# A graph layer's softmax walk: three groups of edges in flight on VectorE instead of two

## The reference

```python
# layer 0: attention over the edges that end in a node, with softmax
h = x @ W
a_src, a_dst = h @ att_src, h @ att_dst
e = leaky_relu(a_src[src] + a_dst[dst], 0.2)      # self loops are added as edges
m = segment_max(e, dst)
e = exp(e - m[dst])
out = segment_sum(h[src] * e / segment_sum(e, dst)[dst], dst)
x = layernorm(x + tanh(out + bias))
# layer 1: h = gelu(x @ W_pre + b_pre); aggr = segment_sum(h[src] * edge_attr, dst)
#          x = layernorm(x + ((x + aggr) + gelu(gelu((x + aggr) @ W1 + b1) @ W2 + b2)))
```

## Time and profile before

| | |
|---|---|
| timed runs, median | 3724.72 us |
| timed runs, all | 3725.86, 3724.72, 3724.6 us |
| span of the profiled execution, first to last instruction | 3722.8 us |
| its own time | not listed apart from the three; the median is 1.9 us above its span |
| GpSimd busy | 2781.1 us (75%) |
| VectorE busy | 2438.3 us (65%) |
| TensorE matmul busy | 2393.6 us (64%) |
| ScalarE busy | 1283.2 us (34%) |

### The profile page before, as it was taken

The page is one execution under the profiler, slowest core; times in us unless marked ns, Lnnn a source line. Parts: engine busy times, 40 slices in busy tenths (PEclk is TensorE's granted clock), DMA queues, the critical chain, the costliest instruction groups (busy, mean ns, idle before and its releaser), DMA issues.

```text
span 3722.8 us, 66966 instructions
## 1 busy us (share of the span) xinstructions
PE 2393.6 (64%) x16704; PEld 1951.7 (52%) x16705; DVE 2438.3 (65%) x6240; ACT 1283.2 (34%) x3893; POOL 2781.1 (75%) x2950
## 2 busy tenths in 40 slices
PE   6433343434344444444445988989888989999888
PEld 3333333333333333333334777777776777777776
DVE  7444444444466666566666777777777788888886
ACT  5433343434445555555553111111111221111222
POOL 7777777777777777777775777777777777777776
PEclk7555555555555555555557999999999999999998
DMA  5222221222222222222223343443334343444332
GB/s 102 43 42 42 41 44 42 44 42 43 42 43 44 43 44 43 43 44 45 44 45 99 93 94 90 95 94 94 95 91 96 93 96 91 97 95 99 93 95 70
DMA packets 351632, 254.26 MB, mean 68 GB/s; under 512 B 254125, under 2 KB 279218, under 8 KB 351387
## 3 DMA queue, kind: packets, MB, share of 16 engines
q0 software_dynamic: 94016, 146.16, 17.8%
q1 hardware_dynamic: 242753, 99.71, 11.7%
q10 hardware_dynamic: 14618, 6.14, 0.6%
HBM read 244.43 MB, written 7.25 MB: 68 GB/s over the span
## 4 chain that ended last, share of the span: by engine, by line
POOL 60%; issue 24%; ACT 4%; DVE 4%; PE 3%; DMA 2%; ACTq 1%; DVEq 1%; POOLq 0%; SPq 0%
POOL rows L690 60%; ACT onehot L747 1%; DMA rows<-table,src_i 1%; DMA src_i<-in_src_dram 1%; PE bank L1086 1%; ACT L790 1%; ACTq L740 0%; ACT pair L767 0%; DVE score L1361 0%; PE bank L1029 0%; PE bank L962 0%; ACT rowu L796 0%; DVE bst L1399 0%; ACT unused L790 0%; DVE newp L1352 0%
## 5 line engine op out<-in xcount | busy, mean ns | idle before, releaser
L690 POOL DMA_INDIRECT rows<-table,src_i x2850 | 2694.8, 946 | 896.0 <-issue 859.5
L1086 PE MATMUL bank<-node,hot 128*128 128x288 bf16 x9310 | 1228.4, 294 | 28.1 <-issue 16.5
L995 PE MATMUL bank<-onehot,rows 128*97 128x72 f32 (+1 forms) x3048 | 584.9, 369 | 814.9 <-ACT onehot L777 814.9
L1086 PEld LDWEIGHTS bank<-node,hot 128*128 128x128 bf16 x9310 | 932.2, 101 | 282.4 <-issue 20.9
L995 PEld LDWEIGHTS bank<-onehot,rows 128*97 128x97 f32 x3048 | 530.8, 281 | 854.4 <-issue 792.5
L1505 DVE TENSOR_SCALAR hot<-node,key 128x642 bf16<-128x642 int16 x1862 | 870.3, 539 | 130.8 <-PE bank L1086 80.0
L900 ACT ACTIVATE pair<-dst_i 128x8 f32<-128x8 int32 x196 | 35.2, 180 | 1175.3 <-DVE rows L1531 904.3
L747 ACT ACTIVATE onehot<-iota,far_dst 128x72 f32 (+1 forms) x1564 | 384.4, 328 | 23.0
L1339 DVE SCALAR_TENSOR_TENSOR other<-onehot,bank 128x576 f32<-128x576 f32 (+1 forms) x196 | 121.9, 622 | 404.1 <-ACT bank L760 335.4
L1073 PE MATMUL bank<-onehot,rows 128*96 128x40 f32 (+1 forms) x3128 | 306.8, 256 | 88.4 <-DVE rows L1536 50.6
L1073 PEld LDWEIGHTS bank<-onehot,rows 128*96 128x96 f32 x3128 | 295.8, 170 | 110.1 <-issue 88.7
(11 more groups left out here) (204 smaller groups left out, 1931.1 us busy)
## 6 DMA issues: line engine op xcount, KB each, us to landing
attr<-in_edge_attr_dram SPq DMA_DIRECT2D x190, 336.0 KB
rows<-table,src_i POOLq DMA_INDIRECT x2850
node<-in_src_dram SPq DMA_DIRECT2D x195, 64.0 KB
attr<-in_edge_attr_dram SPq DMA_DIRECT2D x190, 48.0 KB
dst_i<-in_dst_dram SPq DMA_DIRECT2D x200, 4.0 KB
src_i<-in_src_dram SPq DMA_DIRECT2D x195, 4.0 KB
src_i<-in_src_dram SPq DMA_DIRECT2D x190, 3.5 KB
dst_i<-in_dst_dram SPq DMA_DIRECT2D x190, 3.5 KB
```

The lines of the kernel that those rows point to most:

```text
L690: pool.indirect_dma_start(rows[:, u, j * width:(j + 1) * width], None, table, bass.IndirectOffsetOnAxis(ap=src_i[:, u, j:j + 1], axis=0))\
L995: last = pe.matmul(total[:, 0:w], rows0(u, it)[:, j, 0:D1], wide(weights, w)[:, j, :], start=j == 0, stop=j == most - 1)
L1086: last = pe.matmul(p_got[t], hot[:, c % HOTS, i, t * P:(t + 1) * P], tab[:, a, :, :].rearrange("p k d -> p (k d)"), start=a == 0, stop=a = ...
```

## The change

Layer 0 only. GpSimd's program is the same; SyncE's differs in one semaphore.
- attend on VectorE is cut in pieces. For group g it now does cand and newp, then top_node of g + 1, drop of g, bent (the max with the slope) of g + 1, the subtract and the peak of g, both operations on acc for g - 1, and then started (L1339, L1309 and L1344 before) of g + 2, where it waits for that group's rows. Three groups lead in before the first round.
- ScalarE's weights does newp, fade and weights of g, then given and sloped of g + 2, then away of g + 3.
- away writes into other, of which there is one, and not into onehot; it therefore waits for t0.shift of the group before its own. score has five slots, in the memory of attr, which layer 0 doesn't need.
- TensorE spreads the maxima of g + 1, sums all tiles of g in one go, and turns the maxima of g + 2. A chunk's work on it stands behind the round.
- SyncE waits for the sum (e0.acc) and not for VectorE's add. The buffers of the branch have names of their own.

```diff
-        score = sb("score", [P, TILES * WIN])
+        score = attr[:, :, :].rearrange("p s n -> p (s n)")[:, 0:SLOTS * TILES * WIN].rearrange("p (u n) -> p u n", u=SLOTS)
...
+        def later(g, it, u, k):
+            if it is ROUNDS or (it is ROUNDS - 1 and u + k > SLOTS):
+                return None
+            return g + k, it + (u + k) // SLOTS, (u + k) % SLOTS
...
-                    sp.wait_ge(e.free, g + 1)
+                    sp.wait_ge(e0.acc if e is e0 else e1.free, g + 1)
...
+                act.wait_ge(t0.shift, g + 1)
                 for j in range(tiles_of(g)):
-                    last = act.activation(wide(onehot[:, u, :], w)[:, j, :], iota[:, bass.ds(lo, w)], ACT.Square,
+                    last = act.activation(wide(other, w)[:, j, :], iota[:, bass.ds(lo, w)], ACT.Square,
...
             def weights(g, it, u, ws):
                 w = ws[0]
-                if g is not LAST and u > 0:
-                    away(g + 1, it + (u + 1) // SLOTS, (u + 1) % SLOTS, ws[1])
-                act.wait_ge(t0.shift, g + 2)
-                act.activation(p_slope(w, tiles_of(g)), by_half(score[:, :], w, tiles_of(g)), ACT.Copy, scale=SLOPE).then_inc(t0.slope, 1)
                 act.wait_ge(t0.newp, g + 1)
                 act.activation(p_newp[:, 0:w], newp[:, 0:w], ACT.Copy).then_inc(t0.newpb, 1)
...
+                if later(g, it, u, 2):
+                    given(*later(g, it, u, 2), ws[2])
+                    sloped(*later(g, it, u, 2), ws[2])
+                if later(g, it, u, 3):
+                    away(*later(g, it, u, 3), ws[3])
...
             def attend(g, it, u, ws):
 
                 w = ws[0]
+                if later(g, it, u, 1):
+                    spread_top(t0, g + 2, ws[1], top_diag, p_topb)
...
-                window_sum(p_acc0, onehot[:, u, :], it, u, range(TILES // 2), w)
-                if u == SLOTS - 1:
-                    due(pe, it, middle)
-                spread_top(t0, g + 2, ws[1])
-                window_sum(p_acc0, onehot[:, u, :], it, u, range(TILES // 2, TILES), w).then_inc(e0.acc, 1)
+                window_sum(p_acc0, onehot[:, u, :], it, u, range(tiles_of(g)), w, tiles_of(g)).then_inc(e0.acc, 1)
+                if later(g, it, u, 2):
+                    turn_top(t0, g + 3)
...
+            def started(st, g, it, u, w):
+                v.wait_ge(t0.away, g + 1)
+                v.wait_ge(t0.given, g + 1)
+                n = tiles_of(g)
+                st.link(v.scalar_tensor_tensor(wide(other, w, n), wide(other, w, n), -1.0,
+                                               over_window(p_src, w, n), ALU.mult, ALU.add))
+                largest(t0, other, w, n)
+                v.tensor_tensor(wide(score[:, u, :], w, n), wide(other, w, n), over_tiles(p_dst[:, 0:w], w, n), ALU.add)\
+                    .then_inc(t0.shift, 1)
+            def bent(st, g, it, u, w):
+                n = tiles_of(g)
+                v.wait_ge(t0.slope, g + 1)
+                st.step(v.tensor_tensor(by_half(score[:, u, :], w, n), by_half(score[:, u, :], w, n), p_slope(w, n), ALU.max))
...
+                candidate(st, t0, g + 1, here, w, p_topb)
+                v.tensor_tensor(newp[:, 0:w], cand[:, 0:w], peak[:, here], ALU.max).then_inc(t0.newp, 1)
                 after = None if g is LAST else load_window(g + 1)
+                if later(g, it, u, 1):
+                    top_node(st, t0, g + 2, ws[1], top_diag)
...
                 st.step(v.tensor_tensor(drop[:, 0:w], peak[0:D1, here], newp[0:D1, 0:w], ALU.subtract))
+                if later(g, it, u, 1):
+                    bent(st, *later(g, it, u, 1), ws[1])
+                v.wait_ge(t0.newpb, g + 1)
+                v.tensor_tensor(wide(score[:, u, :], w, n), wide(score[:, u, :], w, n), over_tiles(p_newp[:, 0:w], w, n),
+                                ALU.subtract).then_inc(t0.score, 1)
...
+                if later(g, it, u, 2):
+                    if first(it) and u + 2 < SLOTS:
+                        score_column(u + 2)
+                    started(st, *later(g, it, u, 2), ws[2])
```

More of the change, by code:

```diff
@@ L664, in body @@
                         pool.wait_ge(s_last, 16)
-                        pool.wait_ge(e.free, LAST + 1)
+                        pool.wait_ge(e0.acc if e is e0 else e1.free, LAST + 1)
                         for j in range(LAST_T):
@@ L783, in weights @@
                         act.activation(fade_x[:, 0:w], drop[:, 0:w], ACT.Exp)
[L784 to L786 removed]
+                        act.activation(onehot_x[:, 0:TILES * w], further_score[:, 0:TILES * w], ACT.Exp).then_inc(tx.w, 1)
+                if later(g, it, u, 2):
[3 more added lines that the diff above has]
+                    away(*later(g, it, u, 3), ws[3])
             act.wait_ge(s_const, 5)
@@ L855, in _ @@
             act.wait_ge(a_peak, CHUNKS + RING)
-            given(0, 0, 0, SLIM)
-            away(1, 0, 1, SLIM)
+            for u in range(2):
+                given(u, 0, u, SLIM)
+                sloped(u, 0, u, SLIM)
+                away(u + 1, 0, u + 1, SLIM)
             def middle_due(it):
@@ L1036, in _ @@
             pe.wait_ge(s_w, 16 * 8)
-            spread_top(t0, 1, SLIM)
-            groups(pe, attend, alone=2)
+            turn_top(t0, 1)
+            spread_top(t0, 1, SLIM, top_diag, p_topb)
+            turn_top(t0, 2)
+            groups(pe, attend, middle_due, alone=2)
             def unread(n):
@@ L1306, in scores, with largest @@
                                                over_window(rows0(u, it)[:, :, D1], w), ALU.mult, ALU.add))
-            def largest(t, w, n=TILES):
-                v.tensor_reduce(top[:, 0:w], other[:, 0:n * w].rearrange("p (j n) -> p n j", j=n), AX.X, ALU.max)\
+            def largest(t, of, w, n=TILES):
+                v.tensor_reduce(top[:, 0:w], of[:, 0:n * w].rearrange("p (j n) -> p n j", j=n), AX.X, ALU.max)\
                     .then_inc(t.top, 1)
-            def shift(st, lo, w):
-                st.step(v.tensor_tensor(wide(score, w), wide(other, w), over_tiles(adst[:, bass.ds(lo, w)], w), ALU.add))
@@ L1315, in top_node, with further_shift @@
-            def top_node(st, t, n, w):
+            def further_shift(st, lo, w):
+                st.step(v.tensor_tensor(wide(further_score, w), wide(further_other, w), over_tiles(adst[:, bass.ds(lo, w)], w),
+                                        ALU.add))
+            def top_node(st, t, n, w, diag):
                 v.wait_ge(t.topt, n)
                 st.link(v.tensor_reduce(top_col[0:w, :], p_top[0:w, :], AX.X, ALU.max))
-                v.tensor_scalar(top_diag[0:w, 0:w], ident[0:w, 0:w], top_col[0:w, 0:1], None, ALU.mult)\
+                v.tensor_scalar(diag[0:w, 0:w], ident[0:w, 0:w], top_col[0:w, 0:1], None, ALU.mult)\
@@ L1333, in attend @@
                 lo, further, prev = window(u, "0_" + named(it, u, ws))
-                st = Steps(v, e0.v, g * STEPS0, STEPS0)
-                v.wait_ge(t0.away, g + 1)
-                v.wait_ge(t0.given, g + 1)
+                st = Steps(v, e0.v, AHEAD0 + g * STEPS0, STEPS0)
                 here = bass.ds(lo, w)
                 n = tiles_of(g)
-                st.link(v.scalar_tensor_tensor(wide(other, w, n), wide(onehot[:, u, :], w, n), -1.0,
-                                               over_window(p_src, w, n), ALU.mult, ALU.add))
@@ L1341, in attend @@
-                largest(t0, w, n)
+                candidate(st, t0, g + 1, here, w, p_topb)
+                v.tensor_tensor(newp[:, 0:w], cand[:, 0:w], peak[:, here], ALU.max).then_inc(t0.newp, 1)
                 after = None if g is LAST else load_window(g + 1)
-                v.wait_ge(t0.w, g + 1)
-                v.tensor_tensor(wide(score, w, n), wide(other, w, n), over_tiles(p_dst[:, 0:w], w, n), ALU.add)\
-                    .then_inc(t0.shift, 1)
-                if first(it) and u < SLOTS - 1:
-                    score_column(u + 1)
@@ L1356, in attend @@
+                st.wait()
+                st.step(v.tensor_tensor(peak[:, here], cand[:, 0:w], peak[:, here], ALU.max))
                 before_here = bass.ds(prev, w)
+                v.wait_ge(e0.free, g + SLOTS - 1)
                 st.link(v.tensor_tensor(acc[:, before_here], acc[:, before_here], fade[:, (u - 1) % SLOTS, 0:w], ALU.mult))
-                v.wait_ge(e0.acc, g + 1)
-                v.tensor_tensor(acc[:, before_here], acc[:, before_here], p_acc0[:, 0:w], ALU.add).then_inc(e0.free, 1)
@@ L1360, in attend @@
-                v.wait_ge(t0.newpb, g + 1)
-                v.tensor_tensor(wide(score, w, n), wide(score, w, n), over_tiles(p_newp[:, 0:w], w, n), ALU.subtract)\
-                    .then_inc(t0.score, 1)
-                st.step(v.tensor_tensor(peak[:, here], cand[:, 0:w], peak[:, here], ALU.max))
-                st.done()
+                v.wait_ge(e0.acc, g + SLOTS)
+                v.tensor_tensor(acc[:, before_here], acc[:, before_here], p_acc0[:, 0:w], ALU.add)\
+                    .then_inc(e0.free, 1)
@@ L1478, in _ @@
```

(10 more changed lines are left out.)

80 lines of the change are left out of this document (45 added, 35 removed).

## The result

| | before | after |
|---|---|---|
| timed runs, median | 3724.95 us (4 runs, 3724.6 to 3725.86) | 3741.52 us (4 runs, 3741.23 to 3742.04) |
| ratio | | 1.0043, 95% interval 1.0029 to 1.0058 |
| span of the profiled execution | 3722.8 us | 3739.7 us |

What follows compares the result with a forecast made beforehand. GpSimd's gathers pace the kernel except in its 27.7 us wait at layer 0's end. That end +14.9, stalls 0.5: span 3722.8 to 3738.2, median 3740, plus 1 for register loads: 3741 us; range 3731 to 3757.

Steps and rivals of the forecast that it cites:

- The cycle: Layer 0, one group's round through the engines behind a chunk: 8.18 us against 7.42, with ScalarE's squares in it.
- Rival A: No change: one group's round takes 7.5 us, layer 0 ends +6 us later, 3731 us; decided at 7.6; chance 0.14.
- rival B: Stalls: an exposed register load makes a group's round 8.8 us, GpSimd waits for src_i, 3756 us; chance 0.20.
- The chunk: Layer 0, a chunk's work now stands after the squares: 12.2 us more, so its round takes 53.1 us against 50 of gathering.
- Distance of src_i: Time by which src_i comes ahead of its gathers: 3 us behind a first chunk, none behind a second.
- term for stalls: GpSimd's waits inside layer 0: none counted, but 0.5 us added for rounding.
- remainders: Time a round with a chunk leaves over for the next, 3.1 us each; two put VectorE 6.2 behind at layer 0's end.
- SP's new wait: SyncE's wait for the sum instead of VectorE's add, said to come earlier by that add, with the figures holding this.
- The end: End of layer 0, from group 191 to the last add: 1990.6 against 1975.74 before, so +14.9 us.
- L of 191: Time when the rows of the second group ahead of group 191 are there: 1926.5 + 1.2 = 1927.7.
- drain: Layer 0's last steps after LAST's shift, from bend and subtract through weights and sums to the last adds: + 10.5 us.
- boundary wait: GpSimd's one wait for the stores of table1, at the end of layer 0: from 27.7 to about 42 us.

Runs made afterwards that it cites:

- control run: The change itself, unedited, run beside the variants on a chip where the kernel before takes about 5380 us: 5286.34 us, ratio 0.9817 to the kernel before.

## Why the prediction was right

**The cycle, 8.18 us.** Measured 8.14 to 8.22 behind the chunks of the wide half in the change's profile and 8.13 to 8.25 in the run without gathers. Its reason, the squares between slope and copy, is shown by three edits: off the chain 7.40, behind the copy 7.67, put on the chain of the kernel before 8.4 from 7.42. Rival A (ring under 7.6) falls by the same rows, and rival B (8.8) too: the exposed register load was covered.

**The chunk, + 12.2, round 53.1.** In the wide half a group with a chunk took 20.2 to 20.5 us (8.18 + 12.2 = 20.4 forecast), such a round 53.2, and 53.0 without gathers.

**Distance of src_i: 3 us behind a first chunk, none behind a second.** From SP's issue to the gather, less the forecast's 2 us for landing, it was 3.4 and 0.4 in the two pairs of chunks: right. At the three in a row it was 2.9 behind the first, and behind the second GpSimd stalled; its first late gather began 2.8 us after the issue. The recorded text counts the remainders afresh for the three, but the pair before them left 6 us, and the one free round between (43.9 us of cycles against 50 of gathers) gives back just about that. This time its last group took 11.6 us instead of the usual 11.1, and some 0.5 us were still open when the three began. So the term for stalls, put at 0.5 us, was mis-sized: it measured 2.4. Together with 0.7 us at the start and gathers 1.6 us longer in all, it makes the 4.7 us by which LAST is gathered late; I had counted 0.5. One phrase was too weak as well: SP's new wait comes earlier "by that add". The figures did take the release at the sum, but the add stands 4.7 us behind it in the new order. Subtracted from 3.4 and 0.4 it would have left a stall behind each such chunk; that is an estimate, and was not run on a chip like the first.

**The end.** L of 191 was 1932.3, not 1927.7, and VectorE 4.7 us behind it instead of 6.2; that a part of the remainder vanishes when the rows come late anyway is my reading of it. From there the steps held: 192 with its chunk + 20.2 (20.4), 193 and 194 + 16.1 (16.4), LAST + 6.1 (6.5), drain 9.8 (10.5). The last add ended at 1992.2, where 1990.6 was forecast. The boundary wait was 39.5, "about 42" forecast. So the mechanism held, but that the sum came within 1 us was in part luck: later gathers (+ 4.2 over my figure) and a shorter wait nearly cancel, and the 1 us added for register loads had no counterpart.

**The busiest engine.** GpSimd has the highest share before and after (75% and 74%). By the Trainium skill's rule on the most contended engine (Perfetto Trace Analysis, Identifying the Most-Contended Engine) GpSimd is the engine to work on, and the change touched others. Taken alone, as the only bound, that would have given no cost. It cost 16.6 us: 11.8 through the one wait that others set, the rest because GpSimd came to it later.

**Not the cycle alone.** The 3.0 us behind LAST's start belong to the new order, not to the squares. From that start to the last add it is 8.1 us in every profiled run with the old order (also with the squares on its chain) and 11.1 in every one with the new order (also with the squares off it). The recorded sum has this in its drain and its two groups behind the last rows, but gives it no price of its own.

**What stays open.** How the other 13.5 of the 16.5 us divide between the overrun of each round and the chunk's place behind the start of two more groups. The chunk began 21.4 us later (1939.91 against 1918.47) and needed 5.0 us less to the last add (52.1 against 57.0). By the forecast's steps 12.1 of the 21.4 are its place. By rival A's steps a ring of 7.5 us in the new order would still end at 1982 instead of 1975.7, so of the forecast's 15 us some 6 would be the order's, the drain included, and some 9 the longer cycle's; that is an estimate. The variants that would have shown it, with a cycle of 7.4 or 7.7 us, ran only on chips where that wait can't be read.

## What to carry over

Ahead of a deeper software pipeline, follow one item round the new order and add up the longest chain, with each buffer that there is only one of: here the steady gathers hid a cycle 0.8 us longer everywhere but behind a chunk and at the layer's end. Removing a wait that is hidden gains nothing, while one buffer fewer can put an operation on the chain, and its place in an engine's order decides how much of it (8.2 or 7.67 us with the same one buffer). And when work is put off, look at what returns the ring's slots: taking the release from the sum, not from the postponed add, was worth 169 us of layer 0 where the ring decides.

## What I had not expected of the hardware

The chips differ, or what surrounds them does: the same kernel took 3725 us on one and 5376 to 5508 us on four others, with arithmetic instructions and gathers as long as before. On those the engines stand still for some microseconds, several at once. The largest such waits of VectorE in layer 0 are ahead of top_col (L1344), where one register load from win_tab stands: 658.1 us in 74 times in the control run, put down to "remote" (no instruction is named as releaser). The first chip has some 0.5 us there each time. VectorE and ScalarE in one such group:

```profile
2330.52 0.23 DVE L1382 TENSOR_TENSOR newp<-cand,node 128x72 f32<-128x72 f32 x1
2330.79 0.21 ACT L759 ACTIVATE far_dst<-dst_i 128x8 f32<-128x8 int32 x1
2333.59 2.07 ACT L763 ACTIVATE other<-iota,far_dst 128x72 f32 x8 [2.59 <-issue]
...
2338.72 0.29 DVE L1344 TENSOR_REDUCE top_col<-bank 72x1 f32<-72x128 f32 x1 [7.96 <-remote]
```

In these stretches the engines' own small instructions (register arithmetic and checks, which the busy shares leave out) often take 0.7 us each, on both engines at once: the check behind that load (L1301) takes at most 0.035 us on the first chip and up to 0.71 here. In the two runs without gathers, on such a chip too, no register operation of VectorE or ScalarE takes over 0.5 us from the third round of layer 0 to its last, and the change's cycles are even to 0.1 us (8.13 to 8.25) but for the one at each round's end. So the gaps come with the gathers. Instructions that arrive late would look like this; that they do is not shown. The Trainium skill (Runtime: NRT & Kernel Launch, Instruction fetch mechanics) says that a branch taken out of the fetch window makes the engine wait for a DMA; no run here shows that it is this.

On these chips about every second group of the wide half takes 15 to 18 us instead of 8.2, and GpSimd waits 1514 us for src_i in all, 594 of them in layer 0. The change is 1.8% faster than the kernel before there with the ring released at the sum, and 1.7 to 1.9% slower without that. So its gain there hangs on the release, and the rest of the change loses; whether the kernel before would gain as much from the same release, no run tells. A comparison of two orders thus holds for the conditions in which it was taken.
